# Local attention with its groups turned a step behind their scores, and masks of the causal attention taken off TensorE

## The reference

```
q = l2norm(q) * qs
k = l2norm(k) * ksc
q, k = rotary_xpos(q, k)
sim = jnp.einsum('bhwid,bhwjd->bhwij', bq, bk)
mask = (i < j) | (i > j + WINDOW) | (j == -1)
sim = jnp.where(mask, -jnp.finfo(sim.dtype).max, sim)
attn = jax.nn.softmax(sim, axis=-1)
out = jnp.einsum('bhwij,bhwjd->bhwid', attn, bv)
x = x + o @ wo
```

## Time and profile before

| | |
|---|---|
| time, three runs | 2566.94, 2580.36 (median), 2587.64 us |
| the profiled execution | 2577.56 us, of which the span of the trace is 2575.8 us |
| busy share of the span | PE 75%, weight loads 37%, DVE 53%, ACT 46%, POOL 21% |
| mean granted clock of TensorE | 0.883 of full speed |

### The profile page before, as it was taken

One profiled execution on the slowest core, in us unless ns is written; L12 is line 12 of the kernel. 1 busy time (PEld: TensorE's weight loads), 2 busy tenths in 40 slices (PEclk: granted clock), 3 DMA queues, 4 the chain that ended last, 5 costly groups with the idle time before them and its releaser, 6 DMA issues.

```text
span 2575.8 us, 36677 instructions
## 1 busy us (share of the span) xinstructions
PE 1936.9 (75%) x14096; PEld 962.2 (37%) x14096; DVE 1377.8 (53%) x2359; ACT 1184.5 (46%) x2408; POOL 543.0 (21%) x679
## 2 busy tenths in 40 slices
PE   6786877777787777868689964557898855688985
PEld 2444244433244423443234422223344442244434
DVE  4553465433555345543644367753677544467745
ACT  3454344432444425544524453235477724357762
POOL 2331134200333114320032000001322120223202
PEclk9998999988999799988879987688799977679997
DMA  3000000000000000000043000000444120243402
GB/s 138 1 2 1 0 1 1 2 0 0 1 1 1 1 0 1 1 1 1 0 97 60 3 0 0 0 0 20 97 86 88 26 66 0 49 88 79 86 16 82
DMA packets 50148, 70.81 MB, mean 27 GB/s; under 512 B 4980, under 2 KB 37972, under 8 KB 49464
## 3 DMA queue, kind: packets, MB, share of 16 engines
q1 hardware_dynamic: 47416, 60.07, 10.8%
q0 software_dynamic: 2560, 8.39, 1.2%
HBM read 50.59 MB, written 16.88 MB: 26 GB/s over the span
## 4 chain that ended last, share of the span: by engine, by line
PE 59%; DVE 19%; ACT 10%; issue 6%; POOL 4%; DMA 2%; SPq 0%; POOLq 0%; DVEq 0%; ACTq 0%
PE ps L196 56%; DVE arena L1144 3%; DVE arena L562 3%; ACT arena L509 2%; ACT arena L268 2%; ACT arena L270 2%; PE ps L425 2%; POOL arena L664 1%; POOL arena L657 1%; PE ps L1027 1%; DVE arena L635 1%; ACT arena L518 1%; DVE arena L908 1%; DVE arena L910 1%; DMA arena<-scratch 1%
## 5 line engine op out<-in xcount | busy, mean ns | idle before, releaser
L196 PE MATMUL ps<-arena 128*18 128x256 f32 (+10 forms) x10088 | 719.3, 313 | 196.2 <-DVE arena L1144 47.0
L196 PEld LDWEIGHTS ps<-arena 128*18 128x18 f32 (+6 forms) x10088 | 388.5, 127 | 509.8 <-issue 179.9
L1144 DVE TENSOR_REDUCE arena<-ps 128x2 f32<-128x512 f32 (+1 forms) x640 | 396.9, 661 | 239.2 <-PE ps L196 236.5
L196 PE MATMUL ps<-arena,w_L0f 128*128 128x512 f32 (+3 forms) x800 | 345.9, 569 | 95.9 <-DVE arena L573 28.3
L1128 ACT ACTIVATE arena<-ps 128x1024 f32<-128x1024 f32 (+1 forms) x320 | 313.1, 982 | 134.0 <-PE ps L196 129.6
L509 ACT ACTIVATE arena<-ps,arena 128x128 f32<-128x128 f32 x512 | 227.4, 459 | 112.0 <-DVE arena L606 111.9
L196 PE MATMUL ps<-arena,const 128*32 128x512 f32 (+2 forms) x616 | 228.8, 633 | 44.9 <-ACT arena L1467 19.5
L196 PEld LDWEIGHTS ps<-arena,w_L0f 128*128 128x128 f32 (+2 forms) x800 | 148.0, 201 | 257.2 <-issue 155.5
L664 POOL TENSOR_TENSOR arena<-arena 128x512 f32<-128x512 f32 x128 | 133.0, 1039 | 310.6 <-DVE arena L578 310.6
L562 DVE TENSOR_TENSOR arena<-ps,arena 128x1024 f32<-128x1024 f32 x128 | 152.7, 1220 | 66.8 <-PE ps L196 35.3
L518 ACT ACTIVATE arena<-ps 128x512 f32<-128x512 f32 x128 | 76.0, 598 | 226.2 <-PE ps L196 226.2
(11 more groups left out here) (227 smaller groups left out, 2286.7 us busy)
## 6 DMA issues: line engine op xcount, KB each, us to landing
scratch<-arena SPq DMA_DIRECT2D x40, 384.0 KB, 2.8
arena<-scratch SPq DMA_DIRECT2D x80, 192.0 KB
arena<-scratch SPq DMA_DIRECT2D x80, 128.0 KB
arena<-scratch SPq DMA_DIRECT2D x80, 88.0 KB
w_L0f<-in_L0f SPq DMA_DIRECT2D x2, 1557.0 KB, 12.2
arena<-arena SPq DMA_DIRECT2D x80, 12.0 KB
const<-in_const SPq DMA_DIRECT2D x1, 1276.0 KB, 7.6
residual<-in_x SPq DMA_DIRECT2D x1, 1024.0 KB, 5.0
```

The lines of the kernel that those rows point to most:

```text
L196: return self.nc.tensor.matmul(o, lhsT, rhs, start=start, stop=stop, skip_group_check=True)
L1144: V.tensor_reduce(self.mx[k % 2][:, :, at:at + 1], ps[:, i % 2, 0:SEQ + self.n1].rearrange("p (t s) -> p t s", t=self.blocks), AXX, ALU.ma ...
```

## The change

**Local attention.** (1) Both halves of a group are turned in the step after its scores, so a group is scored and exponentiated in step `G`, and turned and weighed in step `G + 1`; the sum over the heads of a sequence comes one step later, in even steps, and the stage has one more step. (2) Between the two turns, before the first and after the second, PE has one piece of the preparation each; the norm sums move from the end of their step into the next one, after its scores. (3) ACT no longer writes row sums; DVE adds each half of a group (4 rows of 128 columns) before it inverts them. (4) ACT copies the norm columns and POOL limits them to 1e-24 at least and raises them to the power -0.5; the root on ACT and the limit and reciprocal on DVE go. (5) The two exps of a step and the squares stand in another order on ACT.

**Causal attention.** PE adds no mask. DVE adds the mask of a head and takes its maxima in two instructions (128 and 256 columns), each followed by a read of its accumulator, where one reduction stood. POOL sets the masked probabilities of each pair to zero after ACT (`AFFINE_SELECT`), and PE weighs a quad two heads later than before, once POOL has done both its pairs. The two attentions without a mask keep their order.

**Buffers.** `fold` moves into the arena, the arena is larger, and `sums` shares a buffer of the squares. Stages that use them are otherwise as before.

```diff
@@ L0Attend.sum_heads, tensor @@
-        self.wait_ge(eng, self.o_copied, 2 * b + 2)
-        self.wait_ge(eng, self.turn_copied, min(2 * (2 * b + 2) + 2, 2 * self.GROUPS))
+        self.wait_ge(eng, self.o_copied, min(2 * b + 3, self.GROUPS))
...
             if self.live(G):
                 self.score(eng, G)
-            if ahead and r < 2:
-                self.project(eng, c, 4 * r)
-                self.project(eng, c, 4 * r + 1)
-            if ahead and r >= 2:
-                self.value(eng, c, 3 * r - 6)
-                self.value(eng, c, 3 * r - 5)
+            if self.batch_at(G) is not None:
+                self.sum_heads(eng, self.batch_at(G))
+            if r == 1 and ahead:
+                self.norm_sums(eng, c, 0)
+            if r == 2 and ahead:
+                self.norm_sums(eng, c, 1)
+            if ahead:
+                self.piece(eng, c, r, 0)
             if self.live(G - 1):
-                self.turn(eng, 2 * G - 1)
...
+                self.turn(eng, 2 * G - 2)
+            if ahead:
+                self.piece(eng, c, r, 1)
...
-            if self.live(G):
-                self.turn(eng, 2 * G)
+            if self.live(G - 1):
+                self.turn(eng, 2 * G - 1)
+            if ahead:
+                self.piece(eng, c, r, 2)
+            if self.live(G - 1):
+                self.weigh(eng, G - 1)
             if ahead and r < 2:
-                self.norm_sums(eng, c, r)
+                self.piece(eng, c, r, 3)
@@ L0Attend.exps, scalar @@
-                                 scale=rn[:, 2 * (b % PER) + t, 4 * g + j:4 * g + j + 1], accum_out=self.total[G % 2][:, at:at + 1])
+                                 scale=rn[:, 2 * (b % PER) + t, 4 * g + j:4 * g + j + 1])
...
-                S.activation(self.rn[c % 2].rearrange("p x (m d) -> p x m d", m=4), rows, ACT.Sqrt, bias=k.C("zero")).then_inc(self.rooted.sem, 1)
+                S.activation(self.rn[c % 2].rearrange("p x (m d) -> p x m d", m=4), rows, ACT.Copy).then_inc(self.columns_copied.sem, 1)
@@ L0Attend.invert @@
         self.wait_ge(eng, self.exped, q + 1)
+        p4 = self.prob[G % 2][:, 2 * (q % 2):2 * (q % 2) + 2].rearrange("p j t s -> p (j t) s")
+        ch.did(self.k.nc.vector.tensor_reduce(self.total[G % 2][:, at:at + 4], p4, AXX, ALU.add))
+        ch.wait_ge()
         self.k.nc.vector.reciprocal(self.rinv[G % 2][:, at:at + 4], self.total[G % 2][:, at:at + 4]).then_inc(self.inverted.sem, 1)
@@ L0Attend, new @@
+    def invert_norms(self, eng, ch, c):
+
+        rn = self.rn[c % 2]
+        self.wait_ge(eng, self.columns_copied, c + 1)
+        ch.did(self.k.nc.gpsimd.tensor_scalar(rn, rn, 1e-24, None, ALU.max))
+        ch.wait_ge()
+        power = self.k.C("minus_half").unsqueeze(2).to_broadcast([P, 4, 16])
+        self.k.nc.gpsimd.tensor_tensor(rn, rn, power, ALU.pow).then_inc(self.rn_ready.sem, 1)
@@ SmallHeads.quad_at @@
-        w = (s - self.LAG - 5) // 4
-        return w if s % 4 == 2 and 0 <= w < self.QUADS * self.units else None
+        s -= self.LAG + (7 if self.causal else 5)
+        w = s // 4
+        return w if s % 4 == 0 and 0 <= w < self.QUADS * self.units else None
@@ SmallHeads.heads_tensor @@
-                if self.causal:
-                    mm(ps[:, e, 0:3 * P], k_.ident_b[:], k_.mask_q, stop=False)
...
-                if self.causal:
-                    for e in range(2):
-                        mm(ps[:, bank + e, 0:3 * P], k_.ident_b[:], k_.mask_k, stop=False)
...
-                self.wait_ge(eng, self.exped, 2 * w + 2)
+                self.wait_ge(eng, self.selected if self.causal else self.exped, 2 * w + 2)
@@ SmallHeads.heads_vector @@
-                V.tensor_reduce(self.mx[k % 2][:, :, at:at + 1], ps[:, i % 2, 0:SEQ + self.n1].rearrange("p (t s) -> p t s", t=self.blocks), AXX, ALU.max).then_inc(self.topped.sem, 1)
...
+                if self.causal:
+                    for t, (st, end) in enumerate(((0, P), (P, 3 * P))):
+                        o = V.tensor_tensor_reduce(self.masked[:, i % 2, st:end], ps[:, i % 2, st:end], self.k.mask_q[:, st:end], 1.0, MASKED, ALU.add, ALU.max, mx[:, t])
@@ SmallHeads.heads_gpsimd @@
+        for s, k, i in self.steps():
+            g = self.pair_at(s)
+            if self.causal and g is not None:
+                pt = self.pt[g % 4][:, :, 0:3 * P].rearrange("p h (b c) -> p h b c", b=3)[:, :, 0:3:2]
+                self.wait_ge(eng, self.exped, g + 1)
+                G.affine_select(pt, pt, [[0, 2], [0, 2], [1, P]], ALU.is_ge, 0.0, base=0, channel_multiplier=-1).then_inc(self.selected.sem, 1)
```

More of the change, by code:

```diff
@@ L330, in __init__ @@
         self.sq = [a.take(CHUNK) for _ in range(4)]
-        self.sums = a.take(CHUNK)
+        self.sums = self.sq[2]
         self.va = [a.take(3 * INNER).rearrange("p (x c) -> p x c", x=3) for _ in range(3)]
@@ L350, in steps, with batch_at @@
     def steps(self):
-        for G in range(-4, self.GROUPS + 2):
+        for G in range(-4, self.GROUPS + 3):
             yield G, G // 4 + 1, G % 4
+    def batch_at(self, G):
+        return (G - 4) // 2 if G >= 4 and G % 2 == 0 else None
     def live(self, G):
@@ L528, in scalar @@
             ahead = c < NCHUNK
-            if ahead and r < 2:
-                self.square(eng, c, 4 * r)
-                self.square(eng, c, 4 * r + 1)
             if ahead and r == 2:
@@ L536, in scalar @@
                 self.exps(eng, G, 0)
+            if ahead and r < 2:
+                self.square(eng, c, 4 * r)
+                self.square(eng, c, 4 * r + 1)
+            if self.live(G):
+                self.exps(eng, G, 1)
+            if ahead and r == 2:
+                self.wait_ge(eng, self.columned, c + 1)
+                rows = ps[:, 7, :].rearrange("p (x m d) -> p x m d", x=4, m=4)[:, :, :, 0:4]
+                S.activation(self.rn[c % 2].rearrange("p x (m d) -> p x m d", m=4), rows, ACT.Copy).then_inc(self.columns_copied.sem, 1)
             if self.live(G - 1):
@@ L1052, in heads_tensor @@
                 self.wait_ge(eng, self.topped, s - 1)
-                if self.causal:
-                    mm(ps[:, e, 0:3 * P], k_.ident_b[:], k_.mask_q, stop=False)
                 for t in range(2):
                     keys = SEQ if t else self.n1
-                    o = mm(ps[:, e, t * self.n1:t * self.n1 + keys], q[rows, i // 2, t * P:(t + 1) * P], kk[rows, i // 2, 0:keys], start=not self.causal)
+                    o = mm(ps[:, e, t * self.n1:t * self.n1 + keys], q[rows, i // 2, t * P:(t + 1) * P], kk[rows, i // 2, 0:keys])
                 o.then_inc(self.scored.sem, 1)
@@ L1072, in heads_tensor @@
                         rows = slice(64 * e, 64 * e + self.ROWS + PARTS)
-                        o = mm(ps[:, bank + e, at:at + cnt], kk[rows, x, t * P:(t + 1) * P], q[rows, x, st:st + cnt], start=not self.causal)
+                        o = mm(ps[:, bank + e, at:at + cnt], kk[rows, x, t * P:(t + 1) * P], q[rows, x, st:st + cnt])
                 o.then_inc(self.shifted.sem, 1)
@@ L1991, in _ @@
                 nc.gpsimd.memset(k.minus[:], -1.0).then_inc(k.minus_set, 1)
-                eng.wait_ge(k.loaded["const"], 16)
+                for n in ("const", "cols"):
+                    eng.wait_ge(k.loaded[n], 16)
                 for n, s in enumerate(plan):
```

160 lines of the change are left out of this document (74 added, 86 removed).

## The result

The changed kernel takes 2585.35 us (median of 14 runs, 2581.93 to 2591.12), the kernel before 2577.52 us (14 runs). The ratio is 1.0032, 95% interval 1.0018 to 1.0046: within 1%, where 2502 was forecast. The gains of both parts are there, and larger than forecast; one instruction takes them back.

The account below looks back on a forecast made before the run. PE was taken to set the pace, with waits in the local attention and none in the causal; 2577.6 - 53 (local) - 24 (causal) = 2500.6 us profiled, stated as 2502 for the median, range 2460 to 2548.

Parts of the forecast that it names:

- The power on POOL: Local attention's inverse norms: the power over 64 columns takes 1.5 us, hidden up to about 3.5 us.
- rival (1): Local attention: the power on POOL takes long, 2542 us at 6 us, about 2638 at 12; chance 0.10.
- the 77: Whole program: the forecast saving in us, 53 in the local attention and 24 in the causal attention.
- The gain of the local attention: Four local attention stages save 13.3 us each, 53 us in all.
- The walk of one period: Local attention: four steps in the new order sum to 46.9 us, taken as 48.0, against 51.06 before.
- ten or so handovers of about 0.1 us: Local attention: handovers between engines, not in the walk's 46.9 us, bring a period to 48.0 us.
- Its loop through three engines: Local attention, step `r` = 1: DVE 9.3, ACT 3.2 and `weigh` 1.12 make 13.7 us against 13.46; nothing won.
- DVE becomes the bound: Causal attention: DVE needs 15.7 us a unit (0.90 a head), above PE's 12.5 and POOL's 12.9.
- The 3 us for the clock: Causal attention, unit 1: 3 us more at half clock, because PE will be emptier.
- Rival (2): Causal attention: masks win nothing, through slow selections or accumulator reads; 2524 to 2543 us, chance 0.15.
- rival (3): Local attention: DVE's queue costs 0.8 us more a step, so a period's 3.1 us are gone; 2553 us, chance 0.08.
- Rival (4): Local attention: the waits go for good, PE at 43 us a period, 2440 us; chance 0.05.

Follow-up runs that it names:

- the root kernel: The changed kernel with ACT's root and DVE's limit and reciprocal in place of the POOL power: 2456.42 us, ratio 0.9540; on the third chip 2456.38, ratio 0.9549.
- the run with the masks alone: The kernel before with only the causal attention's part of the change (masks on DVE, selections on POOL): 2539.06 us, ratio 0.9853.
- the earlier weighing: The root kernel with the causal attention's weighing two heads earlier, at its place in the kernel before, behind POOL's selection: 2501.57 us, ratio 0.9673.

## Why the prediction was wrong

The step that failed is **"The power on POOL"**: "No row shows one ... I take 1.5 us", and with it the 0.10 for rival (1). The power takes 10.55 us and holds back the widened norms that PE waits for. Rival (1) is what happened. By its own rule (3.5 us hidden, 1 us per us above, 16 times) 10.55 us give 16 x 7.05 = 113 us; measured are 124.5. In full periods the rule is close (7.5 us); at a stage's start nothing is hidden (10.8 us), which the prediction said of the place but not in the sum. The rival's time at that price, 2577 - 77 + 113 = 2613, is 28 above the measured one, since the 77 were too few. (Its "2577 - 77 + 136, about 2638" adds up to 2636; 2638 is 2502 + 136.)

**The gain of the local attention** was 72 us, not 53. The walk of one period (12.5, 13.7, 11.1, 9.6; 46.9 us) met 12.03, 13.76, 11.23, 9.78, together 46.80; that the sum fits to 0.1 us is partly luck, as its steps are off by up to 0.5 us both ways. What failed is the "ten or so handovers of about 0.1 us", which made 48.0 of it. Scores and projection were read as distances between starts, which have handovers in them already; whether that is all of it was not tried. It is 1.2 us a period, 2.4 a stage. The end of a stage was priced at 0.4 us and gave 3.5 (49.94, from 203.31 to 253.25, against 46.40), its start at nothing and gave 2.0 (52.43 against 50.43). A stage in all: 200.8 + 2.0 - 181.5 = 21.3 us instead of 13.3, in the first one. The stages differ; over all four of the same two traces it is 18.4 us a stage (912.2 - 838.7 = 73.5 in all, the measured 72): 8.3 from the two full periods (forecast 6.2), 5.9 from the first one (6.8), 1.8 at the start (0) and 2.4 at the end (0.4).

**Its loop through three engines** was right: step `r` = 1 gained nothing (13.46 before, 13.41 after), and the wait on POOL became one on DVE's queue, forecast at 2 to 3 us in front of the second turn. In the changed kernel, PE and the DVE row in front of it, in order of time:

```profile
186.21 0.68 DVE L581 COPY arena<-ps 128x512 f32<-128x512 f32 x1
186.99 0.63 PE L428 MATMUL ps<-const,arena 128*128 128x128 f32 x4 [2.85 <-issue]
187.45 1.02 PE L195 MATMUL ps<-arena,w_L0f 128*128 128x512 f32 x2
189.47 1.12 PE L195 MATMUL ps<-arena 128*64 128x128 f32 x24 [0.99 <-DVE arena L581]
```

The second turn (186.99) has waited 2.85 us. The row names `issue`, but what ends just before it, at 186.89, is DVE's copy of the first turn (L581), which stands behind a rotation. DVE's sum took 0.676 us (0.68 forecast). That its total is free was right and says nothing of its order: with the sums back on ACT the kernel is 20 us faster.

**The causal attention** gained 38 to 44 us, not 24. "DVE becomes the bound" was wrong. A head was taken at 0.90 us; its two instructions are 0.288 and 0.420, as the slope said, but they start 0.21 and 0.35 us apart, and the accumulator read (0.083) starts with the next instruction:

```profile
1438.13 0.09 DVE L1166 DVE_READ_ACCUMULATOR2_ANT arena<- 128x1 f32 x1
1438.13 0.42 DVE L1166 CUSTOM_DVE_ANT_0 arena<-ps,masks_b 128x256 bf16<-128x256 f32 x1
1438.48 0.09 DVE L1166 DVE_READ_ACCUMULATOR2_ANT arena<- 128x1 f32 x1
1438.48 0.29 DVE L1166 CUSTOM_DVE_ANT_0 arena<-ps,masks_b 128x128 bf16<-128x128 f32 x1
1438.69 0.08 DVE L1166 DVE_READ_ACCUMULATOR2_ANT arena<- 128x1 f32 x1
```

So where nothing holds DVE up a head is 0.56 us from start to start, what the one reduction before took (0.559), and below the 0.71 that was to be the lower end. The sum added full durations that overlap. DVE is busy for 10.46 of a unit's 13.70 us, PE for 11.53, POOL for 9.25; no engine is full, and which chain sets the 13.70 was not taken apart. The selection is 0.637 us, for which I took 1.0. The 3 us for the clock were a size too small at least in some executions: the same causal code took 105.9 us at a mean clock of 0.85, 113.2 at 0.77 and 119.6 at 0.69, and the root kernel alone 105.9 in one execution and 120.2 in another. The last part of the stage, where 4 us were to be saved, took 22.9 us (1468.3 to 1491.2), as before (22.8). The clock ate a part: it was 0.89 there and 1.00 before, and in the run with the masks alone, at 1.00 as before, the same part took 20.5 us (1421.6 to 1442.2), so that 2.3 are saved at an equal clock.

**Rival (2)** (masks win nothing) and **rival (3)** (the order doesn't hold) are excluded by their own experiments, 38 and 72 us. **Rival (4)**, PE at 43 us a period, is excluded by 46.80.

The estimate for compare and select from the GPSIMD Engine Reference of the Trainium skill (Performance pitfalls for Q7 kernels), 0.44 to 0.87 us, holds for the selection: 0.637. Of the 6 us that the same reference gives to a first call (Architecture, Instruction dispatch) the trace shows nothing at the power: the first of the 16 took 10.57 us, the others 10.55 or 10.56, and POOL stood idle for 0.08 us in front of each, the first one too. The rule of VectorE: DVE Perf Modes of the Trainium skill (Rules for kernel authors), to minimize the count of operations, spoke against four instructions in place of one; here they cost the same 0.56 us.

## What to carry to other kernels

A power on POOL costs 0.16 us a column of 128 partitions: price an operation whose kind stands in no row from below and from above, and if there is no upper row, work out at what price it eats the whole gain and put the chance on that. A slow instruction on an in-order queue holds up its own result and whatever stands behind it; ask whether all of it has to come first, as half of it behind the widening gave back 70 of its 124.5 us. When durations overlap, as with DVE's accumulator read, sum distances between starts and not durations. Where the clock differs between executions of one kernel, as it does over the heads here (14 us), price an edit by several runs and not by one stretch.

## What the runs showed of the hardware

The power's time goes by columns: 5.41 to 5.45 us for 32, 10.55 for 64, and the first one in a program costs what the others cost.

POOL and DVE block each other, but not in every instruction. In the kernel before, DVE's copy of 64x510 beside a `scale` of POOL (154.07, 1.04 us) took 1.27 us; in the changed kernel, where POOL's nearest `scale` is over by 112.81, it took 0.42, and so did all 16. Of the 16 in the kernel before, the 8 beside a `scale` took 1.27 each and the 8 with POOL idle 0.42:

```profile
154.12 1.27 DVE L585 COPY arena<-stream 64x510 f32<-64x510 f32 x1
```

```profile
113.39 0.42 DVE L596 COPY arena<-stream 64x510 f32<-64x510 f32 x1
```

This is the exclusive lock of SBUF — State Buffer of the Trainium skill (SBUF: two separate sides), by which the later of the two waits for the whole instruction of the other. Within the power it doesn't hold: DVE's product with two inputs from SBUF (128x8) stands in 12 of the 16 powers, and took 0.17 us in each, as it does alone:

```profile
151.70 0.17 DVE L617 SCALAR_TENSOR_TENSOR arena<-arena 128x8 f32<-128x8 f32 x1
```

Beside an addition of POOL (75.36, 1.27 us) the same product took 1.17 us.

Work taken off PE can come back through its clock. Over the heads of the causal attention the granted clock was 0.89 to 0.94 on average with the masks on PE and PE busy throughout (three traces), 0.69 to 0.85 with the masks gone (nine traces, with 102 to 87 us of PE for the same products), and 0.66 with the earlier weighing. In the changed kernel's second unit, PE busy for 14.16 of 16.50 us, it was 0.50, the lower of its two levels (1.2 GHz).
